# Experts by block of 512 chosen rows instead of all experts for every token, in a two-attention kernel

## What is computed

```
first attention, over the 256 tokens of each of the 32 sequences, 16 heads of 8:
  scores = cov(q, k) / 8 + var(q) var(k) / 8 ; softmax ; times v ; @ Wo
ffn(xn), the second attention and the experts:
  hn = layernorm(xn) ; causal attention of 16 heads of 8, over the 32 SEQUENCES at each of 256 positions
  x1 = xn + attention @ out_proj + bias
  hn2 = layernorm(x1) ; logits = hn2 @ router_w.T (8 experts) ; softmax ; top 2 of 8
  y = sum over the 2 chosen experts e of gate_e * gelu(hn2 @ w1[e]) @ w2[e]     (128 -> 256 -> 128)
  result x1 + y
```

## Time and profile before

| what | value |
|---|---|
| three executions | 1299.87, 1302.8, 1304.02 us (median 1302.8) |
| the profiled execution, and its span | 1300.59 us, 1298.3 us |
| PE busy (matmul), weight loads | 1127.0 us (87%), 669.0 us |
| DVE, ACT, POOL busy | 989.6, 796.9, 375.9 us |
| DMA traffic | 24.90 MB, 19 GB/s |
| chain of waits, by engine | PE 43%, POOL 19%, ACT 17%, issue 11%, DVE 8% |

### The profile page before, as it was taken

The page is one execution under the profiler, slowest core; times in us unless marked ns, Lnnn a source line. Parts: engine busy times, 40 slices in busy tenths (PEclk is TensorE's granted clock), DMA queues, the critical chain, the costliest instruction groups (busy, mean ns, idle before and its releaser), DMA issues.

```text
span 1298.3 us, 33300 instructions
## 1 busy us (share of the span) xinstructions
PE 1127.0 (87%) x11462; PEld 669.0 (52%) x11462; DVE 989.6 (76%) x2827; ACT 796.9 (61%) x1440; POOL 375.9 (29%) x644
## 2 busy tenths in 40 slices
PE   1498888888888888888769999999999999999998
PEld 0234444444444444443236666666666666666676
DVE  2767887888888888876467888787888887897773
ACT  0046665666666666666647666777667677667744
POOL 5343554444445555540021011111011110011000
PEclk9999997999999999997778999999999999999999
DMA  3000000000000000000010110000000000000000
GB/s 95 5 10 15 15 17 17 17 17 17 13 17 13 17 17 17 17 11 27 5 46 1 26 26 6 20 24 24 24 19 5 24 24 24 24 11 14 18 10 17
DMA packets 50452, 24.90 MB, mean 19 GB/s; under 512 B 5984, under 2 KB 49888, under 8 KB 50400
## 3 DMA queue, kind: packets, MB, share of 16 engines
q1 hardware_dynamic: 50400, 24.21, 6.9%
HBM read 15.28 MB, written 8.39 MB: 18 GB/s over the span
## 4 chain that ended last, share of the span: by engine, by line
PE 43%; POOL 19%; ACT 17%; issue 11%; DVE 8%; ACTq 1%; POOLq 0%; DMA 0%; SPq 0%; DVEq 0%
PE bank L558 39%; ACT Kexp L1383 7%; ACT hmid L1458 4%; POOL xn L431 4%; POOL stack L461 3%; ACT prob L1361 3%; POOL sq L443 2%; DVE smax L1053 2%; PE bank L599 2%; POOL rstd L428 2%; POOL sq L445 2%; POOL stack L456 2%; ACT prob L1394 1%; POOL feat L453 1%; DVE prob L1057 1%
## 5 line engine op out<-in xcount | busy, mean ns | idle before, releaser
L975 DVE TENSOR_REDUCE rowmin<-bank 128x2 f32<-128x512 f32 x512 | 336.9, 687 | 119.0 <-PE bank L558 114.7
L1361 ACT ACTIVATE prob<-bank 128x512 f32<-128x512 f32 x512 | 301.4, 607 | 204.8 <-PE bank L558 203.8
L558 PEld LDWEIGHTS bank<-w_sb,hmid 128*128 128x128 f32 x2048 | 244.0, 192 | 24.1 <-issue 12.3
L558 PE MATMUL bank<-w_sb,hmid 128*128 128x128 f32 x2048 | 248.5, 276 | 0.2 <-issue 0.2
L1458 ACT ACTIVATE hmid<-bank,up_scale 128x512 f32<-128x512 f32 x256 | 175.9, 732 | 111.3 <-PE bank L558 111.1
L558 PE MATMUL bank<-QKT 32*128 32x256 f16 x2048 | 199.4, 285 | 31.9 <-ACT prob L1361 15.4
L1383 ACT ACTIVATE Kexp<-bank,head_bias,head_mask 128x512 f32<-128x512 f32 x256 | 187.8, 846 | 42.5 <-PE bank L558 42.5
L1266 DVE SCALAR_TENSOR_TENSOR acc<-bank,gate,acc 128x128 f32<-128x128 f32 x512 | 143.3, 342 | 72.9 <-PE bank L558 70.8
L487 POOL TENSOR_TENSOR rstd<-mv,epsilon 128x4 f32<-128x4 f32 x16 | 8.9, 553 | 503.9 <-DVE mv L1204 503.9
L558 PEld LDWEIGHTS bank<-QKT 32*128 32x128 f16 x2048 | 68.0, 94 | 155.6 <-issue 68.4
L558 PE MATMUL bank<-prob,V 128*25 128x256 f32 x2048 | 147.3, 408 | 0.0
(11 more groups left out here) (177 smaller groups left out, 1622.4 us busy)
## 6 DMA issues: line engine op xcount, KB each, us to landing
x_in<-in_L_attn_x SPq DMA_DIRECT2D x32, 128.0 KB, 2.1
z_scratch<-z_out SPq DMA_DIRECT2D x32, 128.0 KB, 1.8
xg<-in_L_attn_x SPq DMA_DIRECT2D x64, 64.0 KB, 2.0
zg<-z_scratch SPq DMA_DIRECT2D x64, 64.0 KB, 1.9
out<-acc SPq DMA_DIRECT2D x64, 64.0 KB, 1.6
QKT<-shiftT SPq DMA_DIRECT2D x128, 4.0 KB
w_sb<-in_L_ffn_w SPq DMA_DIRECT2D x1, 1024.0 KB, 6.1
wo<-in_L_attn_Wo SPq DMA_DIRECT2D x16, 4.0 KB
```

What stands on the lines that cost most here:

```text
L558: return pe.matmul(o, l, r, start=start, stop=stop, skip_group_check=True)
L975: dve.tensor_reduce(rowmin[h // 8][:, :, h % TILE_ROWS, h // TILE_ROWS % HALF], row_scores[i % 3][:].rearrange("p (s t) -> p s t", s=ST), ...
L1361: act.activation(prob[:, h % 8].rearrange("p t s -> p (t s)"), col_scores[h % 2][:], ACT.Exp, scale=exp_register).then_inc(s_exp, 1)
```

## The change

The order of the stages is turned round, and the experts get a stage of their own.

1. **Groups** (16, POOL, PE, DVE, ACT, SP `group_step`): the second attention alone. For each group the router's two best experts are found, `ranks` (PE) and `make_spots` (DVE) give each of the 1024 pairs a row number in the list of its expert, and POOL writes the rows (hn2 in two float16 parts and the gate, 516 bytes) to `token_rows` in HBM by 8 indirect DMAs of 128 rows (`scatter`). SP also stores `x + x1` (`out_base`) and the row numbers (`places`). The keys are now spread over 4 partition quadrants with 4 activations instead of 16, and the scores of a group are 64 products of 32 x 32 x 128.
2. **Blocks**: 40 blocks (`BLOCKS` = 16384 / 512 + 8) of 512 rows. SP reads the block's first row and its expert from a table into registers (`value_load`), loads 512 token rows and one expert's weights (258 and 257 KB), PE turns the rows, runs the same six and eight matmuls, DVE multiplies by the gate and SP stores 256 KB to `expert_out`. Rows beyond the end of a list are blank; all 40 blocks always run. Three buffers (`XBUFS`) hold the loads.
3. **First attention** as before, but with POOL's `combine(b - 2)` and `gather(b)` in each step: the output is `z + out_base +` the two rows of `expert_out` that `place` names, gathered by 4 indirect DMAs of 128 rows. It is stored by `store_out` straight to the result. Its first two preparing steps run before the blocks.

The diff, cut to the parts that the steps below speak of:

```diff
+H2_TOP, W1_TOP = 2.0 ** 4, 2.0 ** 14
+
+
+TOPK = 2
...
+BLOCKS = TOPK * NB * NS // BLK + NE
...
+XBUFS = 3
...
-    return tuple(0 <= g + d < GROUPS for d in range(4))
+    return tuple(0 <= g + d < GROUPS for d in (-1, 0, 1, 2))
...
-        z_dram = nc.dram_tensor("z_scratch", (NB, NS, E), F32).ap()
+        out_base = nc.dram_tensor("out_base", (NB, NS, E), F32).ap()
+        token_rows = nc.dram_tensor("token_rows", (XROWS, ROWW // 2), U32).ap()
+        expert_out = nc.dram_tensor("expert_out", (XROWS, E), U32).ap()
+        weight_rows = nc.dram_tensor("weight_rows", (NE * P, WROW // 2), U32).ap()
...
+            def scatter(n, p, lo, hi):
+
+                if lo == 0:
+                    pool.wait_ge(s_spot, n + 1)
+                    pool.tensor_tensor(spare[:], epsilon[0:1, 0:1], epsilon[0:1, 0:1], ALU.add)
+                for j in range(lo, hi):
+                    pool.indirect_dma_start(token_rows, bass.IndirectOffsetOnAxis(spots[p][:, j:j + 1], 0),
+                                            rows[p][:, j // TILES, j % TILES, :].bitcast(U32), None).then_inc(s_scat[p], 16)
+
...
+                if norm:
+                    scales(g + 2)
+                if late:
+                    scatter(g - 1, 1 - p, 0, 3)
+                if tail:
+                    scales2(g)
+                if late:
+                    scatter(g - 1, 1 - p, 3, COLS)
+                if tail:
+                    add_x(g, p)
+                    low_part(g, p)
+                if isinstance(g, int) and g == -2:
...
+            def gather(n, p):
+
+                if isinstance(n, int) and n == 0:
+                    for k in range(2):
+                        pool.wait_ge(s_yd[k], 16 * BLOCKS // 2)
+                pool.wait_ge(s_based[p], n * 16 + (32 - 16 * p))
+                if positive(n - 1):
+                    pool.wait_ge(s_comb, n - 1)
+                pool.tensor_tensor(spare[:], epsilon[0:1, 0:1], epsilon[0:1, 0:1], ALU.add)
+                for k in range(TOPK):
+                    for st in range(ST):
+                        pool.indirect_dma_start(ysel[p][:, k, st, :].bitcast(U32), None, expert_out,
+                                                bass.IndirectOffsetOnAxis(place[p][:, st, k:k + 1], 0)
+                                                ).then_inc(s_sel[p], 16)
+
+            def combine(n, p):
+
+                pool.wait_ge(s_z, n + 1)
+                pool.wait_ge(s_sel[p], n * 32 + (64 - 32 * p))
+                pool.tensor_tensor(base_t[p][:], base_t[p][:], ysel[p][:, 0], ALU.add).then_inc(s_pool, 1)
+                pool.wait_ge(s_pool, own.next())
+                pool.tensor_tensor(base_t[p][:], base_t[p][:], ysel[p][:, 1], ALU.add).then_inc(s_pool, 1)
+                pool.wait_ge(s_pool, own.next())
+                pool.tensor_tensor(z_out[p][:], z_out[p][:], base_t[p][:], ALU.add).then_inc(s_comb, 1)
...
                     normalise_x(b + 3, 1 - p)
                     features_stack(b + 3)
-                if isinstance(b, int) and NB - 2 <= b < NB:
-                    scales(b - (NB - 2))
+                if not (isinstance(b, int) and not 0 <= b - 2 < NB):
+                    combine(b - 2, p)
+                if cur:
+                    gather(b, p)
...
+            def causal_scores(n):
+
+                pe.wait_ge(s_kexp, n + 1)
+                if positive(4 * n):
+                    pe.wait_ge(s_sdiff, 4 * n)
+                for r in range(QUAD):
+                    part = slice(r * SEQ, (r + 1) * SEQ)
+                    mm(quad_scores[r][:], seq_eye[part].rearrange("k q s -> k (q s)"),
+                       causal[part].rearrange("k h t -> k (h t)"), stop=False)
+                for t in range(TILES):
+                    for q in range(QUAD):
+                        c = t * P + q * SEQ
+                        for r in range(QUAD):
+                            part = slice(r * SEQ, (r + 1) * SEQ)
+                            ins = mm(quad_scores[r][q * SEQ:(q + 1) * SEQ, t * P:(t + 1) * P],
+                                     gqT[part, c:c + SEQ],
+                                     Kexp[part, t * QUAD + q].rearrange("p j t -> p (j t)"), start=False)
+                            if t == TILES - 1 and q == QUAD - 1:
+                                ins.then_inc(s_sc, 1)
...
+            def ranks(n):
+
+                pe.wait_ge(s_pick, n + 1)
+                mm(tail_bank[:, 0:(COLS + 1) * NE], below[:], pick[:].rearrange("p j e -> p (j e)"), stop=False)
+                for j in range(COLS):
+                    ins = mm(tail_bank[:, (j + 1) * NE:(COLS + 1) * NE].rearrange("p (j e) -> p j e", e=NE), onesb[:],
+                             pick[:, j:j + 1, :].broadcast_to([P, COLS - j, NE]), start=False, stop=(j == COLS - 1))
+                ins.then_inc(s_rank, 1)
...
+            def turn(i):
+                pe.wait_ge(s_bx[i % XBUFS], 32 * (i // XBUFS + 1))
+                if i >= 2:
+                    pe.wait_ge(s_turned, i - 1)
+                m = turn_bank[i % 2][:].bitcast(F16)
+                for a in range(2):
+                    for st in range(SUBS):
+                        ins = pe.transpose(m[:, a * BLK + st * P:a * BLK + (st + 1) * P],
+                                           xrow[i % XBUFS][:, st, a * E:(a + 1) * E], identh[:])
+                ins.then_inc(s_turn_ps, 1)
+
...
+                pe.wait_ge(s_feat, 2)
+                pe.wait_ge(s_max, 4)
+                turn(0)
+                for i in range(BLOCKS):
+                    expert_up(i)
+                    if i + 1 < BLOCKS:
+                        turn(i + 1)
+                    if i >= 1:
+                        expert_down(i - 1)
+                expert_down(BLOCKS - 1)
...
+                if tail:
+                    block_transposes(g)
+                if head:
+                    take_q(g + 1)
+                if late:
+                    choose(g - 1)
...
+                    attention_scales()
+                if late:
+                    second_rows(g - 1, 1 - p)
+                    make_spots(g - 1, 1 - p)
+                if tail:
+                    causal_normalise(g)
+                if head:
+                    score_maxima(g + 1, 0, 2)
+                if tail:
+                    make_x1(g, p)
+                if head:
+                    score_maxima(g + 1, 2, 4)
+                if tail:
+                    high_part(g, p)
...
+            def expert_y(i):
+                dve.wait_ge(s_down, i + 1)
+                if i >= 2:
+                    dve.wait_ge(s_yd[i % 2], 16 * (i // 2))
+                gates = xrow[i % XBUFS][:, :, GATE:GATE + 2].bitcast(F32)
+                dve.tensor_tensor(y_sb[i % 2][:], down_bank[i % 2][:].rearrange("p (s e) -> p s e", s=SUBS),
+                                  gates.broadcast_to([P, SUBS, E]), ALU.mult).then_inc(s_y, 1)
...
-            def store_z(b, p):
-                sp.wait_ge(s_z, b + 1)
-                sp.dma_start(z_dram[b].rearrange("(s p) e -> p s e", p=P), z_out[p][:]).then_inc(s_zd[p], 16)
...
+            def load_base(b, p):
+                if positive(b - 1):
+                    sp.wait_ge(s_comb, b - 1)
+                with nc.allow_non_contiguous_dma(reason="two places of a token"):
+                    sp.dma_start(place[p][:], places[:, b, :].rearrange("(s p) k -> p s k", p=P)).then_inc(s_based[p], 16)
+                sp.dma_start(base_t[p][:], out_base[b].rearrange("(s p) e -> p s e", p=P)).then_inc(s_based[p], 16)
+
+            def store_out(b, p):
+                sp.wait_ge(s_comb, b + 1)
+                sp.dma_start(out[b].rearrange("(s p) e -> p s e", p=P), z_out[p][:]).then_inc(s_out[p], 16)
...
+            def load_block(i):
+
+                k = i % XBUFS
+                if i >= XBUFS:
+                    sp.wait_ge(s_y, i - XBUFS + 1)
+                at = sp.value_load(table[0:1, 0, i:i + 1], min_val=0, max_val=XROWS - BLK)
+                of = sp.value_load(table[0:1, 1, i:i + 1], min_val=0, max_val=(NE - 1) * P)
+                sp.dma_start(xrow[k][:].bitcast(U32), token_rows[bass.ds(at, BLK), :].rearrange("(s p) c -> p s c", p=P)
+                             ).then_inc(s_bx[k], 16)
+                sp.dma_start(wrow[k][:].bitcast(U32), weight_rows[bass.ds(of, P), :]).then_inc(s_bx[k], 16)
+
+            def store_block(i):
+                sp.wait_ge(s_y, i + 1)
+                at = sp.value_load(table[0:1, 0, i:i + 1], min_val=0, max_val=XROWS - BLK)
+                sp.dma_start(expert_out[bass.ds(at, BLK), :].rearrange("(s p) e -> p s e", p=P),
+                             y_sb[i % 2][:].bitcast(U32)).then_inc(s_yd[i % 2], 16)
...
+                for i in range(BLOCKS):
+                    if i + XBUFS - 1 < BLOCKS:
+                        load_block(i + XBUFS - 1)
+                    store_block(i)
...
                     place_shift(b + 1, 1 - p, 0)
-                if prev:
-                    store_z(b - 1, 1 - p)
```

(38 more changed lines are left out.)

1293 lines of the change are left out of this document (687 added, 606 removed).

## The result

The changed kernel takes **1943.3 us** (median of 4 runs, 1929.6 to 1950.2); the kernel before, beside it, 1301.3 us (4 runs). The ratio is 1.493, 95% interval 1.483 to 1.502: slower by half. The prediction was 1800 us with a range of 1450 to 2080. The profiled execution has a span of 1938.8 us.

A forecast was written before the change was run, and what follows sets the result against it. Before the change PE bound the groups and a ring through POOL the first attention, 17.03 us per batch. Groups 422, table and first attention steps 28, blocks 400, attention 953: 1803 us of span, said as 1800, range 1450 to 2080.

The forecast's parts named there:

- POOL's 7.90 us of idle time: First attention, kernel before: POOL's wait per batch from its normalisation's end until PE's next slot 0 releases it.
- the ring: First attention: PE's slot 0, POOL's stack and normalisation, PE's slots 9 to 16; 17.03 us, plus 11.6 added.
- round trip: Attention, between combine and gather: POOL waits for loads SP issues behind combine, store and shifts; 4.2 us per batch.
- the two clocks: PE's higher and lower (1.2 GHz) levels: attention batch 28.6 us at the higher, 32.7 at the lower.
- PE's part: Attention: PE's share of the batch, shortened if ACT and DVE catch up by slot 9; blocks: turn 0.6, down 2.0 us.
- The wait at L610: Attention, a sign: POOL waits 3 to 4 us there on base_t's load.
- cheap indirect DMAs and a hidden round trip: Rival, 1420 us, chance 0.15: an indirect DMA holds POOL 0.4 us, loads land meanwhile; batch 21.2 us.
- The ring through three buffers: Blocks: y of block i releases load i + 3, whose turn precedes the down giving the next y; 10 us per block.
- The landing: Blocks: time for a block's loads to arrive, with the store 770 KB, half under the issues; about 4 us.
- The ring through POOL: Groups: scales2, five indirect DMAs, additions, DVE, normalisation, PE and ACT steps, make_x1; 22 us, taken as 23 per group.
- It all hides (1155): Rival, chance 0.05: POOL's idle time is real room, attention keeps 17.03 us per batch, groups 20, blocks 4.3.
- Everything at its dear end (2190): Rival, chance 0.10: indirect DMA 2.03 us, PE at its low level; batches 36 us, groups 28, blocks 13.

The follow-up runs named there:

- early_combine: Changed kernel with POOL doing combine and gather between normalisation and the next stack, SP's order left as it was: 1850.9 us.
- no_gather: Changed kernel without the four indirect DMAs per batch that fetch the experts' rows; the additions stay and add zeros: 1805.1 us.
- down_first: Changed kernel, blocks only, three buffers, PE doing down of block i - 1 ahead of the turn of block i + 1: 1847.3 us.
- four_buffers: Changed kernel with XBUFS = 4 instead of 3 for the blocks' rows and weights, nothing else: 1713.1 us.
- scatter_late: store_later with all eight indirect DMAs of a group behind scales2 on POOL, instead of three ahead of it: 1936.5 us.
- store_later: Changed kernel, group loop only: SP issues the store of a group's sum one step later, behind the next load of x: 1936.3 us.
- best_try: all_three with combine's additions on DVE, five block buffers, late loads and blank stores issued later, PE's next-group work ahead of h2's turn: 1241.4 us, ratio 0.954.
- half_gather: all_three with two of a gather's four indirect DMAs; the second expert's rows are left out and zeros added: 1295.1 us.
- early_places: early_combine plus places loaded one step ahead, base rows later for combine only, both shift loads ahead of the output's store: 1695.6 us.
- all_three: Changed kernel with early_places, store_later and four_buffers together: 1443.4 us, ratio 1.111 to the kernel before.

## Why the prediction was right, point by point

**Sign and mechanism of the attention: right.** I said that POOL's 7.90 us of idle time stand behind its work and in front of its release, so that work put between stack and normalisation lengthens the ring. early_combine shows just that: same instructions, other place, 4 us less. The terms: combine 2.3 (2.4 predicted), round trip 4.7 (4.2), gather 5.2 (5.0); batch 31.4 (30, between the 28.6 and 32.7 given for the two clocks). My reason for 30, that ACT and DVE would have caught up and shorten PE's part, did not come: POOL waited 9.4 to 10.6 us for slot 0, where the earlier trace rows had 7.9. The wait at L610 was to be 3 to 4 us and is 4.7; PE's wait for xn about 10 and is 7.4 after 3.2 spent on the shifts. That the shifts cost nothing as long as the ring is longer held.

The indirect DMA was the term with no row: between 0.40 and 2.03 I took 1.2, and it is 1.26 (0.96 and a pause of 0.30; 128 of each kind). The Trainium skill (DMA: Bandwidth & Descriptors, Anatomy of one DMA — SWDGE path) has the generating of descriptors as a small part of a DMA, of which many fit before a cost shows. For POOL's time the trace does not agree: 128 rows take 1.26 us of it, some 320 us over the run, and no_gather gave back 4.8 of the 5.2 us that a gather had cost. What of it is per row stays open, since every indirect DMA here has 128. The rival *cheap indirect DMAs and a hidden round trip* failed on both of its conditions.

**Blocks: right mechanism, sizes off both ways.** The ring through three buffers is what down_first and four_buffers cut. The register loads took twice what I gave them: 1.8 us for 0.9. The Trainium skill's price (same page, Latency and other measured facts), a floor of about 600 ns for one, gives 1.8 for three, but as a floor it is not borne out: the load itself took 0.26 to 0.55 us, with the register work behind it 0.5, 0.5 and 0.8. The landing was too dear (2.9 for 4.0), and in us PE's part was furthest off (4.6 for 2.6, lower clock). Together 11.4 for 10, and 440 us for 400.

**Groups: the wrong ring.** Here a step failed. I wrote "The ring through POOL: `scales2` 2.3, five indirect DMAs at 1.2" and on through PE and ACT to 22 us. The trace closes over SP instead: I did not ask what SP has queued behind the store that POOL's last addition releases. It is the next load of x. And cutting that ring showed no gain clear of the spread (26.0 us per group for 26.2), since PE's queue at the lower clock with 6.6 us of waiting is nearly as long (24.4). scatter_late, which puts eight indirect DMAs behind `scales2` where my ring counted five, takes the same time as store_later, so my ring does not set the group; best_try, which gives PE other work in the place of that wait, has groups of 23.6 us. Both rings are above 23, and 16 times 3.2 is 51 of the 81 us. The other 30 are the start, where I took 15 us for loads and masks: SP's 24 issues and PE's bias products hold DVE 14.8 and 8.0 us.

**Other rivals.** *It all hides (1155)* would have broken even at 5.5 us added per batch; it was 12.2. It was wrong for this kernel, but the 17.03 us that it kept can nearly be had: half_gather, with half of the rows left out, has the batch at 17.0, and best_try at 17.5 us at its shortest, 18.6 in the mean. *Everything at its dear end (2190)* wanted indirect DMAs of 2.03 us.

**The clock.** I charged the lower level in part, and it was granted almost everywhere (0.69 to 0.72). early_places shows that it then outlives the ring: with POOL out of the way a batch still took 21.6 us, PE being granted 0.68 to 0.83 (and 1 us per batch lay in the pauses with DVE and ACT). What lets it rise is open in part: with PE busy 83 to 87% it was 0.68 to 0.83 in early_places, and in the attention of the kernel before, in one window,

```profile
33.00:651.00 618.00, 511.60 (x5418) 247.53 (x5418) 472.15 (x1020) 370.09 (x787) 270.22 (x447) 0.96 0.05 15
```

0.96 with PE busy 83%. The busy share of a stage does not tell the two apart.

## What to carry to other kernels

Idle time of an engine is room only if it stands between the work that you add and its own next release; write down the ring (who releases whom, in which order on each queue) and put new work where the engine waits for the others, with its inputs loaded a step ahead. Look at what stands behind a store on the queue that issues it: a load that nothing needs to hold back may be waiting for the slowest engine. And cut the rings one by one, but a single cut may give nothing, as in the groups here, where the next ring lay just below; in the blocks one more buffer gave 230 us.

## What the runs showed of the hardware that I had not expected

An indirect DMA of 128 rows holds POOL 0.95 us (the first of a row 1.1 to 1.2) and keeps the next one away 0.30 us more, nearly alike for a scatter of rows of 516 bytes and a gather of rows of 512. A load of one register from a tile in SP's queue takes 0.26 to 0.55 us, with the register work behind it 0.5 to 0.8.

In all_three DVE and ACT paused together, mostly for 2.1 to 2.4 us, near the end of POOL's four indirect DMAs, with the scores that they read written by PE's modelled ends and the profile naming no engine of the core ("remote"); early_places has 15 such pauses too. With two DMAs, or with all four earlier and the additions on DVE, it was not there. What holds them was not settled, a late PE included: no run here moved the DMAs and nothing else.
